# A bf16 matmul of 512 columns behind each aggregation of a graph network's second message stage

## The chip, the core and the metric

The kernel runs on one core of a Trainium2 chip. A core has five engines with instruction streams of their own: TensorE (PE, matrix products into PSUM), VectorE (DVE), ScalarE (ACT), GpSimd (POOL) and SyncE (SP), and 16 DMA engines that move data between HBM and on-chip memory (SBUF). Engines meet only at semaphores. The metric is the device time of one execution in microseconds (us); the median of three runs is given.

## The reference

Two layers of message passing on a graph of 6250 nodes with 256 features and 106250 edges, sorted by destination. Cut to what matters:

```python
# layer 0: a message network per edge, summed per node, then an update network
msg = silu(concat(h[src], h[dst], w) @ mW1 + mb1)
msg = silu(layer_norm(msg) @ mW2 + mb2)
agg = segment_sum(msg, src, 6250)
x = layernorm(x + x + mlp(concat(x, agg)))
# layer 1: the mean over the incoming edges, one projection
agg = segment_sum(x[src], dst, 6250) / max(count, 1)
x = layernorm(x + relu(agg @ W.T + b))
```

The change lies in layer 1's `segment_sum(x[src], dst)`, the second message stage.

## The kernel before

Edges are cut into 831 tiles of 128 (`TILES`), 832 with padding, and nodes into 50 blocks of 125 (`BLOCKS`, `NB`). Since edges are sorted by destination, a tile touches one block or a few neighbouring ones. Each pair of a tile and a block is a *visit*; there are 880 (`VISITS`), in 220 quads of four (`QUADS`, `QT`). The program runs its stages one after the other: preparation of the index tables, the first message stage (until about 3030 us), the update of the nodes in blocks, the second message stage (about 3290 to 4576 us) and the projection with the last norm.

In the second message stage three engines work in a ring, and all synchronisation is by hand.

- **GpSimd** (L498 to L507) issues one indirect DMA per tile: it gathers 128 rows of `x1_tab` from HBM into one of 64 slots of `ring`. The code is unrolled. From the sixteenth tile on, gather `t` waits on the semaphore `agg` until 15 fewer visits than its number are aggregated: `pool.wait_ge(e[1]["agg"], tile - (RING - BEHIND) + 1)`. GpSimd can so be about 15 tiles ahead.
- **PE** (`aggregate`, L720 to L738) loads four slot numbers into registers, waits for the one-hot matrices of the quad (`hot`) and for the quad's four gathers (`s_ring`), and then, for each visit `u` of the quad, waits until VectorE has emptied PSUM bank `u` of the visit four places back (`acc`) and multiplies the one-hot matrix `same1` (128 edges x 125 nodes, fp32) with the gathered rows (128 x 257, fp32, the last column is a one that counts edges). This matmul releases `agg`. In the trace one such fp32 matmul is two MATMUL instructions, so L736 has 1760 of them for 880 visits. The loop of the chip's program holds four quads.
- **VectorE** builds the next quad's four one-hot matrices (`one_hot_1`, L1328), reads four block numbers into registers, and then for each visit waits for `agg` and adds the PSUM bank to the rows of that block in SBUF (`accumulate`, L1341), which releases `acc`.

PSUM has eight banks of 512 fp32 columns. The stage uses banks 0 to 3 for the four visits of a quad. Bank 6 (`PK`) is used in earlier stages and by nobody in this one. `identh` is a 128 x 128 identity matrix in bf16, filled at the start of the program. ScalarE does nothing in this stage.

Of the kernel before, what the change touches and what calls it, by code (L numbers as in the profile page):

```python
# [17 lines left out]
P = 128  # L18
# [3 lines left out]
QT = 4  # L22
# [27 lines left out]
def gnn(nc, x, src, dst, edge_w, mW1, mb1, ln_g, ln_b, mW2, mb2, uW1, ub1, uW2, ub2, W, b, out):  # L50
# [11 lines left out]
    with ExitStack() as ctx:  # L62
        def sb(name, shape, dt=f32):
            return ctx.enter_context(nc.sbuf_tensor(name, shape, dt))
# [6 lines left out]
        identh = sb("identh", [P, P], bf16)  # L71
# [138 lines left out]
        ps = ctx.enter_context(nc.psum_tensor("ps", [P, 7, 512], f32))  # L210
        psh = ctx.enter_context(nc.psum_tensor("psh", [P, QT, P], bf16))
        PM, PZ, PP, PK = 0, 2, 4, 6
# [70 lines left out]
        def later(q, n):  # L283

            return not isinstance(q, int) or q >= n
# [225 lines left out]
        def _(pe):  # L511
# [31 lines left out]
            for c in range(CHUNKS):  # L543
                pe.wait_ge(s_done_g, c + 1)
                for v in range(2):
                    last = nc.tensor.matmul(ps[:, v, 0:HV], onesf[:, :], pick[:, c % 2, 0, v * HV:(v + 1) * HV],
                                            start=c == 0, stop=c == CHUNKS - 1)
# [4 lines left out]
            for c in range(CHUNKS):  # L552
                pe.wait_ge(s_pick, 2 * (c + 1))
                for a in range(3):
                    edges = ends[:, a, c, :] if a < 2 else loaded[:, 2, c, :]
                    for v in range(2):
                        last = nc.tensor.matmul(ps[:, 2 * a + v, 0:HV], edges, pick[:, c % 2, 0, v * HV:(v + 1) * HV],
                                                start=c == 0, stop=c == CHUNKS - 1)
# [166 lines left out]
            def aggregate(q, k_):  # L725

                par = k_ % 2
                pe.load(slot_regs, vslot[0:1, bass.ds(q * QT, QT)])
                at = [pe.snap(reg, min_val=0, max_val=RING - 1) for reg in slot_regs]
                pe.wait_ge(e[1]["hot"], q + 1)  # L730
                if not isinstance(q, int) or q < TILE_QUADS:
                    pe.wait_ge(s_ring[k_], (q // 4 + 1) * (16 * QT))
                for u in range(QT):
                    if later(q, 1):
                        pe.wait_ge(e[1]["acc"], (q - 1) * QT + u + 1)
                    nc.tensor.matmul(ps[0:NB, u, 0:CW], same1[:, par, u, :],  # L736
                                     ring[:, bass.ds(at[u], 1), :].rearrange("p a c -> p (a c)"),
                                     start=True, stop=True).then_inc(e[1]["agg"], 1)  # L738
            pe.wait_ge(s_slots, 5)
            pe.wait_ge(s_ones, 1)  # L740
            for q in range(4):
                aggregate(q, q)
            with pe.Fori(1, TILE_QUADS // 4) as it:
                for k_ in range(4):
                    aggregate(it * 4 + k_, k_)
            for q in range(TILE_QUADS // 4 * 4, QUADS):
                aggregate(q, q % 4)
# [649 lines left out]
```

## Time and profile before

| | |
|---|---|
| median of 3 runs | 4703.93 us |
| lowest and highest run | 4698.99 and 4730.17 us |
| the profiled execution's own time | 4717.16 us |
| its span, first to last instruction | 4715.4 us |
| PE busy | 3347.0 us (71%) |
| VectorE busy | 2799.7 us (59%) |
| GpSimd busy | 3095.4 us (66%) |
| ScalarE busy | 1598.1 us (34%) |

A row of the profile's trace names a line of the kernel, an engine and an operation, with the tiles it writes and reads (`ps<-arena`: PSUM from SBUF; the big arrays all lie in `arena`). PEld is PE's weight load, which runs beside its matmuls. An engine's name with a q (DVEq) is its sequencer: register operations, waits and branches. Such rows are not counted as busy time. "idle before" is the time the engine stood still ahead of an instruction, and the arrow behind it names what ended it; "issue" there means that no wait which the profile shows ended it. Matmuls overlap in the array, so the duration of one is longer than its share of the time. The granted clock is the share of 2.4 GHz that TensorE was given; its two levels are 0.5 and 1.0.

### The profile page before, as it was taken

How to read it: one execution, taken by the hardware profiler on the slowest of the kernel's cores; microseconds unless marked ns; L12 is line 12 of the kernel's file. 1: busy time of each engine (PE TensorE's matmuls, PEld its weight loads, DVE VectorE, ACT ScalarE, POOL GpSimd, SP SyncE). 2: the span in 40 equal slices, each digit the busy share in tenths (PEclk: the TensorE clock that was granted, in tenths of full speed). 3: DMA queues.
4: the chain of work that ended last, by engine and by line, in shares of the span. 5: the costliest groups of instructions: out<-in, count | busy, mean ns of one | idle time of the engine just before them, and what ended most of it. 6: DMA issues, size and time to landing. Idle time of an engine off the chain costs nothing. (4 is left out here: it accounts for less than half of the span.)

```text
span 4715.4 us, 78508 instructions
## 1 busy us (share of the span) xinstructions
PE 3347.0 (71%) x16589; PEld 2444.8 (52%) x16590; DVE 2799.7 (59%) x13402; ACT 1598.1 (34%) x2993; POOL 3095.4 (66%) x2666
## 2 busy tenths in 40 slices
PE   6777777878887777787778777695555555555564
PEld 3366666666666666666666666574222323223232
DVE  4466666666666666666666666577444444444466
ACT  0355555555555545555555555431000000000001
POOL 0078888888888788878887888612666666666620
PEclk8988899898888988989898888897666676666688
DMA  8345555555555555555555555654333233323213
GB/s 278 100 78 83 83 82 83 83 84 82 83 83 83 82 83 82 83 83 83 82 83 82 83 83 83 123 162 135 88 87 87 85 89 88 89 86 90 86 45 100
DMA packets 311717, 437.83 MB, mean 93 GB/s; under 512 B 49696, under 2 KB 256636, under 8 KB 311420
## 3 DMA queue, kind: packets, MB, share of 16 engines
q0 software_dynamic: 208896, 339.90, 38.6%
q1 hardware_dynamic: 102524, 95.40, 6.8%
q14 instruction: 285, 2.33, 0.2%
q8 instruction: 12, 0.20, 0.0%
HBM read 273.86 MB, written 161.01 MB: 92 GB/s over the span
## 5 line engine op out<-in xcount | busy, mean ns | idle before, releaser
L475 POOL DMA_INDIRECT sum<-arena,sidx x880 | 1403.1, 1594 | 304.2 <-issue 258.8
L463 POOL DMA_INDIRECT arena<-p_tab,idx x880 | 863.2, 981 | 489.7 <-issue 254.4
L736 PE MATMUL ps<-arena 128*125 x1760 | 721.2, 547 | 611.0 <-DVE arena L1341 323.9
L504 POOL DMA_INDIRECT arena<-x_tab,esrc x832 | 796.6, 957 | 500.4 <-PE ps L736 222.3
L648 PE MATMUL ps<-w,arena 128*128 128x256 f32 x3520 | 885.0, 384 | 15.6 <-issue 7.6
L736 PEld LDWEIGHTS ps<-arena 128*125 128x125 f32 x1760 | 391.1, 255 | 941.1 <-issue 892.2
L1341 DVE TENSOR_TENSOR arena<-ps,arena 125x257 f32 x880 | 375.0, 426 | 600.0 <-issue 419.4
L613 PE MATMUL ps<-arena 128*128 128x256 f32 x1760 | 607.2, 506 | 109.1 <-ACT arena L840 106.8
L648 PEld LDWEIGHTS ps<-w,arena 128*128 128x128 f32 x3520 | 601.0, 191 | 149.0 <-issue 25.6
L822 ACT ACTIVATE arena<-ps,key 128x128 f32<-128x128 f32 x880 | 251.5, 369 | 1130.8 <-remote 1081.9
L623 PE MATMUL ps<-ident,arena 128*128 128x128 f32 x1760 | 280.0, 310 | 457.1 <-DVE arena L1173 404.2
L613 PEld LDWEIGHTS ps<-arena 128*128 128x128 f32 x1760 | 434.2, 259 | 222.5 <-issue 145.0
L900 ACT ACTIVATE arena<-ps 128x250 f32<-128x250 f32 x50 | 19.0, 382 | 1418.0 <-PE ps L756 1418.0
L623 PEld LDWEIGHTS ps<-ident,arena 128*128 128x128 f32 x1760 | 218.9, 157 | 493.0 <-DVE arena L1173 347.2
L1150 DVE BATCH_NORM_STATS2 bst<-arena 128x6 f32<-128x256 f32 x880 | 330.7, 418 | 236.4 <-ACT arena L812 204.6
L636 PE MATMUL ps<-arena 128*128 x2640 | 361.6, 291 | 5.7 <-DVE arena L1140 4.9
L1140 DVE TENSOR_TENSOR arena<-ps,arena 128x512 f32<-128x512 f32 x440 | 281.3, 679 | 141.2 <-PE ps L623 59.5
L833 ACT ACTIVATE arena<-ps,gb 128x512 f32<-128x512 f32 x440 | 341.8, 777 | 0.0
L1173 DVE TENSOR_SCALAR arena<-arena,mom,nwt 128x256 f32<-128x256 f32 x880 | 321.0, 426 | 34.8 <-DVE nwt L306 26.5
L636 PEld LDWEIGHTS ps<-arena 128*128 128x128 bf16 x2640 | 279.8, 106 | 100.0 <-issue 29.8
L812 ACT ACTIVATE arena<-arena 128x512 f32<-128x512 f32 x440 | 276.7, 629 | 46.3 <-DVE arena L1140 46.1
L1328 DVE TENSOR_SCALAR arena<-nodes,vloc 128x125 f32<-128x125 bf16 x880 | 202.8, 299 | 121.1 <-issue 66.3
(175 smaller groups left out, 4285.7 us busy)
## 6 DMA issues: line engine op xcount, KB each, us to landing
sum<-zeros SPq DMA_DIRECT2D x4, 6400.0 KB
arena<-sum SPq DMA_DIRECT2D x200, 128.0 KB, 2.1
arena<-p_tab,idx POOLq DMA_INDIRECT x880
sum<-arena,sidx POOLq DMA_INDIRECT x880
arena<-x_tab,esrc POOLq DMA_INDIRECT x832
arena<-x_tab SPq DMA_DIRECT2D x50, 128.0 KB, 2.0
pxin<-in_x_dram SPq DMA_DIRECT2D x50, 112.0 KB
p_tab<-prow SPq DMA_DIRECT2D x50, 112.0 KB
```

The source lines that it names most:

```text
L463: pool.indirect_dma_start(out=gat[:, par, u, 0:D], out_offset=None, in_=p_tab[:, :], in_offset=bass.IndirectOffsetOnAxis(ap=idx[:, par, u: ...
L475: pool.indirect_dma_start(out=sums[u][:, :], in_=tot[:, par, u, :], in_offset=None, out_offset=bass.IndirectOffsetOnAxis(ap=sidx[:, par, u ...
L504: pool.indirect_dma_start(out=ring[:, tile % RING, 0:D], out_offset=None, in_=x1_tab[:, :], in_offset=bass.IndirectOffsetOnAxis(ap=esrc[:, ...
L613: last = nc.tensor.matmul(ps[:, PM + u // 2, u % 2 * D:(u % 2 + 1) * D], same[:, par, u, :], msg[:, par, u, 0:D], start=True, stop=True)
L623: last = nc.tensor.transpose(ps[:, PZ + h, u * P:(u + 1) * P], act[:, par, u, h * P:(h + 1) * P], ident[:, :])
L636: last = nc.tensor.matmul(ps[:, PP + u // 2, u % 2 * D:(u % 2 + 1) * D], hott[:, par, u, :], big[:, bass.ds(blocks_[u], 1), i, :].rearrang ...
L648: nc.tensor.matmul(to, zt[:, par, h, u * P:(u + 1) * P], w2[:, h, :], start=h == 0, stop=False)
L736: nc.tensor.matmul(ps[0:NB, u, 0:CW], same1[:, par, u, :], ring[:, bass.ds(at[u], 1), :].rearrange("p a c -> p (a c)"), start=True, stop=T ...
L833: nc.scalar.activation(zt[:, par, h, :], ps[:, PZ + h, :], ACT.Identity, bias=gb[:, h, 1:2], scale=gb[:, h, 0:1]).then_inc(s["zev"], 1)
L1150: nc.vector.bn_stats(bst[:, par, u, :], act[:, par, u, :]).then_inc(s["bst"], 1)
L1173: last = nc.vector.tensor_scalar(act[:, par, u, :], act[:, par, u, :], m[:, 4, u:u + 1], nwt[:, par, 3, u:u + 1], ALU.subtract, ALU.mult)
L1341: nc.vector.tensor_tensor(row, ps[0:NB, u, 0:CW], row, ALU.add).then_inc(s["acc"], 1)
```

## The change

Behind the aggregation of each visit PE runs one more matmul. Its stationary operand is `identh`, its moving operand is `identh` read four times over (512 columns, bf16), and it writes all of PSUM bank 6, which nothing in this stage reads or writes otherwise. It waits for no semaphore and releases none. The aggregation's own release of `agg` stays where it was, ahead of it. Everything else is as it was.

```diff
                     nc.tensor.matmul(ps[0:NB, u, 0:CW], same1[:, par, u, :],
                                      ring[:, bass.ds(at[u], 1), :].rearrange("p a c -> p (a c)"),
                                      start=True, stop=True).then_inc(e[1]["agg"], 1)
+                    nc.tensor.matmul(ps[:, PK, :], identh[:, :], identh[:, :].unsqueeze(1).to_broadcast([P, QT, P]),
+                                     start=True, stop=True)
```

On PE, inside a quad of the second message stage, the program reads as follows (ISA rows are register operations and waits, `arena` is the one-hot matrix and the ring). Before:

```order
L728 TENSOR_LOAD vslot
L729 ISA
L736 ISA [waits e1_acc,s_ring1,e1_hot]
L736 MATMUL ps<-arena 125x257
L736 ISA [waits e1_acc]
L736 MATMUL ps<-arena 125x257
```

And with the change, where L739 is the added matmul:

```order
L728 TENSOR_LOAD vslot
L729 ISA
L736 ISA [waits e1_acc,s_ring1,e1_hot]
L736 MATMUL ps<-arena 125x257
L739 MATMUL ps<-identh 128x512
L736 ISA [waits e1_acc]
L736 MATMUL ps<-arena 125x257
L739 MATMUL ps<-identh 128x512
```

Each pair of a wait and an aggregation has one matmul more behind it, ahead of the wait for the next visit's bank. No other engine's instructions move.

## Rows read from the trace of the kernel before

**Rows 1.** The page: span; granted clock in tenths, 40 slices.
```profile
span 4715.4 us, 78508 instructions
...
PEclk8988899898888988989898888897666676666688
```

**Rows 2.** Stretches of the run: length, busy time (count) by engine, granted clock, DMA share, GB/s.
```profile
3290.00:4522.00 1232.00, 677.13 (x1626) 369.38 (x1627) 526.19 (x1628) 0.00 (x0) 787.01 (x823) 0.68 0.30 88
4523.00:4576.00 53.00, 39.30 (x125) 18.47 (x123) 38.29 (x123) 0.00 (x0) 0.50 (x1) 0.99 0.02 4
```

**Rows 3.** The line view of L736: durations min/median/max, then waits.
```profile
L736 PE MATMUL ps<-arena x1760: 377/534/790, 3285.9 to 4574.7; 128*125 x196
...
  DVE arena L1341: 323.9, 161
...
  POOL arena L504: 222.3, 269
```

**Rows 4.** The line view of L504 (the gathers of the stage).
```profile
L504 POOL DMA_INDIRECT arena<-x_tab,esrc x832: 951/957/1043, 3279.0 to 4522.5; - x167
...
  PE ps L736: 222.3, 269
```

**Rows 5.** The line view of L1341; DVEq is VectorE's sequencer.
```profile
L1341 DVEq FUSED_REGOPS  x880: 2/57/1410, 3292.8 to 4576.4; - x176
L1341 DVE TENSOR_TENSOR arena<-ps,arena x880: 421/426/429, 3292.9 to 4576.5; 125x257 f32 x176
...
  issue: 419.4, 369
```

**Rows 6.** Timeline, a fast stretch: start, duration, engine, line, count, idle before.
```profile
3811.44 9.39 PE L736 MATMUL ps<-arena 128*125 x24 [1.77 <-DVE arena L1341]
...
3814.19 0.95 POOL L504 DMA_INDIRECT arena<-x_tab,esrc  x1 [0.30 <-issue]
3814.26 0.43 DVE L1341 TENSOR_TENSOR arena<-ps,arena 125x257 f32 x1 [0.27 <-issue]
...
3815.45 0.96 POOL L504 DMA_INDIRECT arena<-x_tab,esrc  x1 [0.31 <-PE ps L736]
...
3817.65 0.43 DVE L1341 TENSOR_TENSOR arena<-ps,arena 125x257 f32 x1 [0.28 <-issue]
```

**Rows 7.** Timeline, the slow stretch that follows.
```profile
3825.08 0.42 DVE L1341 TENSOR_TENSOR arena<-ps,arena 125x257 f32 x1 [3.27 <-issue]
...
3825.66 1.21 PE L736 MATMUL ps<-arena 128*125 x2 [4.83 <-issue]
...
3827.19 0.43 DVE L1341 TENSOR_TENSOR arena<-ps,arena 125x257 f32 x1 [1.68 <-issue]
...
3829.28 0.43 DVE L1341 TENSOR_TENSOR arena<-ps,arena 125x257 f32 x1 [1.67 <-PE ps L736]
3829.51 0.95 POOL L504 DMA_INDIRECT arena<-x_tab,esrc  x1 [1.77 <-PE ps L736]
```

**Rows 8.** Stretches: three cycles, each a fast stretch and the slow one after it.
```profile
3808.60:3831.40 22.80, 14.32 (x34) 8.29 (x34) 10.22 (x32) 0.00 (x0) 14.32 (x15) 0.65 0.29 83
3952.70:3976.30 23.60, 14.56 (x34) 7.91 (x32) 10.13 (x32) 0.00 (x0) 15.28 (x16) 0.64 0.30 86
3831.40:3847.40 16.00, 7.38 (x20) 4.50 (x19) 7.09 (x22) 0.00 (x0) 10.51 (x11) 0.71 0.32 95
```

**Rows 9.** Stretches: the matmuls of L736 alone, inside one fast stretch.
```profile
3811.40:3817.00 5.60, 5.56 (x13) 4.21 (x14) 0.50 0.28 83
3817.50:3820.40 2.90, 2.79 (x10) 1.34 (x9) 1.00 0.33 105
```

**Rows 10.** Line view of L636 (bf16, 256 columns), one quad; its stretch.
```profile
L636 PE MATMUL ps<-arena x12: 272/272/273, 507.1 to 508.3; 128*128 x12
...
506.50:508.60 2.10, 1.46 (x12) 1.18 (x12) 0.99 0.40 105
```

**Rows 11.** A stretch after the last gather.
```profile
4530.00:4570.00 40.00, 29.00 (x94) 13.47 (x92) 29.11 (x95) 0.00 (x0) 0.00 (x0) 1.00 0.00 0
```

## The prediction

> **What bounds the kernel now.** I first located the stage, then asked who waits for whom in it, then looked at a timeline to see in what rhythm the waits come. The page gives a span of 4715.4 us and a row of granted clock whose digits are 8 and 9 up to the last third and 6 and 7 through the second message stage [rows 1]. The stage runs from about 3290 us. Until the last gather at 4522.5 us it takes 1232 us, and then 53 us more [rows 2]. In the 1232 us no engine is full: PE is busy 677 us, VectorE 526 us and GpSimd 787 us, at a mean clock of 0.68.
>
> The three engines form a ring. GpSimd issues 832 gathers, from 3279.0 to 4522.5 us, each 0.957 us long [rows 4]. Back to back they start 1.26 us apart (3814.19 and 3815.45) [rows 6], so unhindered they would need 832 x 1.26 = 1048 us. They take 1243.5 us, 1.495 us each, and GpSimd spends 222.3 us waiting for PE [rows 3, 4]. PE in turn waits 323.9 us for the accumulation of L1341 [rows 3]. What the accumulation waits for is the point of the case: of VectorE's idle time before it, 419.4 us is put down to "issue", that is, to nothing the profile shows as a wait, and its sequencer's register operation, 57 ns in the median, takes up to 1410 ns [rows 5].
>
> The timeline shows two alternating states. In a **fast stretch** a quad of four tiles takes VectorE 3817.65 - 3814.26 = 3.39 us, 0.85 us a tile, and PE runs without a break for 9.39 us [rows 6]. In a **slow stretch** accumulations of 0.43 us start 2.1 us apart (3825.08, 3827.19, 3829.28), though the matmul for each was long done; GpSimd streams on until its credit of slots is used up and then stands idle for 1.77 us [rows 7]. After such a pause VectorE is fast again. Why its sequencer slows I can't tell from this trace. What I can read is what it costs on average: three whole cycles, of 22.8, 23.6 and 16.0 us, hold 15, 16 and 11 gathers [rows 8], which makes 1.52, 1.48 and 1.45 us a gather. A short cycle and a long one cost the same per tile. So I treat about 1.5 us a tile as the stage's pace, set between VectorE's sequencer and GpSimd, and not by PE.
>
> **What the change adds.** One matmul and one weight load behind each of the 880 aggregations, nothing removed, nothing moved, no wait, no DMA. The nearest row for the matmul is the bf16 matmul of 256 columns in the first message stage: at a clock of 0.99 twelve of them start within 1.2 us (507.1 to 508.3), 0.11 us apart [rows 10]. 512 columns are then 0.22 us at full clock. The granted clock has two levels here, 1.2 and 2.4 GHz, so at the lower one it is 0.43 us. Its weight load stands beside the stream in those same rows, so I put it at nothing; if it does not hide, it is up to 0.1 us a tile more, and the cover below has room for that.
>
> The aggregation itself: at 0.50 of the clock 13 matmuls (two make one tile) fill 5.56 us, 0.43 us each, 0.86 us a tile; at full clock at most 2.79 / 10 = 0.28 us each, 0.56 us a tile, and that with waits in it [rows 9]. With the added matmul PE needs 0.86 + 0.43 = 1.29 us a tile at the lower clock and at most 0.56 + 0.22 = 0.78 us at the upper one.
>
> Term 1, PE's time. 0.68 of the clock means that (0.68 - 0.5) / 0.5 = 36% of the stage is at the upper level, so the mean price is 0.36 x 0.22 + 0.64 x 0.43 = 0.35 us, times 880 = 312 us of engine time. PE has 1232 - 677 = 555 us idle before the last gather [rows 2]. It fits. If the idle time went away, the 312 us would lie open, but the next terms say where it could.
>
> Term 2, fast stretches at the upper clock: 0.78 us is under VectorE's 0.85. Nothing.
>
> Term 3, fast stretches at the lower clock. 1.29 us is more than 0.85, so here PE takes over from VectorE. After a slow stretch PE starts at 0.50 of the clock and stays there for about 6 us (3811.4 to 3817.0 is at 0.50, 3817.5 on at 1.00) [rows 9]. That is 7 tiles, each 0.43 us later: 3.0 us a cycle. With three cycles of 20.8 us in the mean there are 1232 / 20.8 = 59 of them, 177 us in all, if nothing takes it up.
>
> What takes it up: GpSimd is ahead of PE. Gather t waits only for aggregation t - 15. At 1.29 us a tile PE is just about as fast as GpSimd's 1.26, so GpSimd isn't starved in those 6 us; it merely keeps less credit for the slow stretch that follows, uses it up sooner, pauses sooner, and the pause is what ends the slow stretch. The cycle gets shorter, and the cost per tile does not depend on its length [rows 8]. The pace of 1.5 us also stays above 1.29. The spread between the three cycles, 1.45 to 1.52, is 5%, so it can hide some of a loss; I take a tenth of the 177 us, 17 us, as not absorbed, and keep 0 and 177 as bounds.
>
> Term 4, slow stretches. VectorE takes 2.1 us a tile and PE, at 0.50, has 1.21 us of visible matmul time per tile there [rows 7]; 1.21 + 0.43 = 1.64 is still under 2.1. Since four PSUM banks let PE run four tiles ahead, the added matmul isn't in the loop. Nothing.
>
> Term 5, after the last gather: 94 matmuls in 40 us at clock 1.00, that is 0.85 us a tile, VectorE busy 29.1 of 40 us [rows 11]. PE's 0.78 fits. At most a cold first quad, 4 x 0.43 = 2 us. I take 1.
>
> **Sum.** 0 + 17 + 0 + 1 = 18 us, call it 16 to 20. The profiled execution took 4717.2 us (span 4715.4); the median of the runs shown is 4703.9, 13 us less. Against the median: 4704 + 16 = 4720 us. One per cent, 47 us, is what I count as a difference that a measurement can tell.
>
> **Rivals.**
> *The slow stretches keep their length (slower).* Place: the first six microseconds of each fast stretch. If a slow stretch ends after a fixed time, or needs a pause of GpSimd that comes no sooner, term 3 isn't absorbed: 177 us, 4881 us; half of it, 4793 us. It decides from the point at which GpSimd's wait for PE grows from 222 us. For it: PE is really over VectorE's pace there, 1.29 to 0.85. Against: the three cycles' equal price, and GpSimd's lead. Chance 0.28 for anything over 47 us.
>
> *An even pace (faster).* At 1.29 us PE would hold VectorE near GpSimd's own rhythm, and if VectorE's sequencer only slows after it has run 0.85 us a tile beside a streaming GpSimd, slow stretches get rarer. The limit is 832 x 1.29 = 1073 us instead of 1243.5, so -170 us, 4534 us; half, 4619 us. Against: the clock rises after 6 us and PE is then fast again. Chance 0.12.
>
> *The clock (faster).* In a slow stretch the clock falls, and the next fast one begins at 0.50 [rows 9]; the added columns might keep it up. Then the 1.21 us per tile of slow stretches would be nearer to 1.21 - 0.43 = 0.78. With some 3 such tiles in each of 59 cycles, and if all of it were in the loop, 59 x 3 x 0.43 = 76 us, 4628 us. Against: with VectorE at 2.1 us a tile and PE four tiles ahead it is not in the loop, and in fast stretches PE's 0.86 cold equals VectorE's 0.85. The Trainium skill ("TensorE: Matmul & The Clock Gate", "Why this matters for your kernels") says that gaps between matmul bursts throw PE back to the lower clock, and advises to keep it busy. By that rule the added matmul makes the aggregations faster; the trace agrees about the clock (0.50 after a slow stretch) and speaks against the gain. Chance 0.08.
>
> That the matmul doesn't run at all is excluded by the program's order, where it stands behind every aggregation.
>
> **Chances and range.** My forecast, within 1%: 0.52. Slower 0.28. Faster 0.12 + 0.08 = 0.20. The time is that of the forecast, 4720 us. The range reaches down to the half of the even pace, 4620 us, and up to 0.8 of term 3 unabsorbed, 4704 + 142 = 4846, say 4850 us; about 0.08 lies below and 0.10 above. The forecast's own range is 4690 to 4750 us.
>
> **What would show it.** Right: 880 matmuls of 512 columns; fast stretches that begin at 1.29 us a tile at 0.50 of the clock; cycles shorter than 20.8 us with about 1.5 us a gather; GpSimd's wait for PE near 222 us; the gathers' first to last start near 1243 us; 0.85 us a tile after the last gather. Wrong, slower: the same 10 us slow stretches behind longer fast ones, and PE waiting for VectorE less while GpSimd waits for PE more. Wrong, faster: few accumulations 2 us apart, and gathers 1.26 to 1.3 us apart throughout. A clock near 1.0 in the whole stage with the same time would show the clock's rival to be about the clock alone.

## The result, and the profile after

The changed kernel takes 4661.5 us (median of 4 runs, 4658.0 to 4663.4) against 4704.3 us before: 0.990 of it, 95% interval 0.987 to 0.993. That is 43 us, 0.9 to 1.0%, faster. I had forecast 4720 us and no change. The time lies inside the wide range (4620 to 4850 us), by the room that the rivals had been given, and outside the forecast's own 4690 to 4750 us; the direction was clear of noise and I had missed it. Measured again, on a later occasion, it was 4684.6 against 4718.3 us, 0.993 (0.992 to 0.995).

The profiled execution's span fell by 56 us, from 4715.4 to 4659.4 us. The line view of the gathers says where it went; columns as in [rows 4].

```profile
L504 POOL DMA_INDIRECT arena<-x_tab,esrc x832: 947/953/1040, 3266.0 to 4470.1; - x167
...
  issue: 194.2, 628
  remote: 137.9, 74
  PE ps L736: 79.4, 129
```

The gathers' first to last start now takes 4470.1 - 3266.0 = 1204.1 us, where it took 1243.5: 39 us, 1.449 us a gather instead of 1.495. 13 us were already gone when the first gather started, ahead of anything that the change touches (the profiled execution of before was itself 13 us over the median), and 4 us after the last. So the gain lies where the added matmul lies, ahead of the last gather. The second pair of traces gives 40 us there (1253.0 and 1212.9 us).

The stretch view of the message stage and of its tail, columns as in [rows 2]:

```profile
3277.00:4470.00 1193.00, 792.41 (x2451) 464.11 (x2450) 523.77 (x1633) 0.00 (x0) 784.03 (x823) 0.77 0.31 90
4471.00:4523.00 52.00, 42.95 (x180) 26.73 (x179) 37.73 (x121) 0.00 (x0) 0.02 (x1) 0.99 0.03 4
```

The line view of the added matmul, columns as in [rows 3]:

```profile
L739 PE MATMUL ps<-identh x880: 377/379/634, 3273.9 to 4520.7; 128*128 128x512 bf16 x176
```

PE's busy time and its clock rose (0.68 to 0.77) and the tail after the last gather kept its length [rows 2]. What the added matmul costs PE came out as estimated. A timeline at 0.5 of the clock shows it, columns as in [rows 6]:

```profile
3720.12 0.63 PE L739 MATMUL ps<-identh 128*128 128x512 bf16 x1
3720.55 1.07 PE L736 MATMUL ps<-arena 128*125 x2
3721.40 0.63 PE L739 MATMUL ps<-identh 128*128 128x512 bf16 x1
...
3722.68 0.63 PE L739 MATMUL ps<-identh 128*128 128x512 bf16 x1
```

One tile takes PE 3722.68 - 3721.40 = 1.28 us (I had 1.29), and the added matmul 3720.55 - 3720.12 = 0.43 us. At full clock (0.98 from 3683.0 to 3685.6) a tile takes 3685.13 - 3684.48 = 0.65 us (rows below; I had at most 0.78).

The reader should now compare what VectorE's accumulation waits for with [rows 5]:

```profile
L1343 DVEq FUSED_REGOPS  x880: 3/57/1410, 3279.9 to 4522.0; - x176
L1343 DVE TENSOR_TENSOR arena<-ps,arena x880: 416/426/429, 3280.0 to 4522.2; 125x257 f32 x176
...
  remote: 214.5, 76
  PE ps L736: 206.2, 250
  issue: 136.7, 211
```

"issue" fell from 419.4 to 136.7 us, and "remote", 14.2 us before, is 214.5 us. Part of that is a matter of records: the trace of before holds 677 updates of the semaphore `agg` for its 880 visits, that of after 791, and where the update has no record the profile can name nobody and says "issue". The timeline shows what hides behind "remote":

```profile
3684.05 0.60 PE L736 MATMUL ps<-arena 128*125 x2
...
3684.48 0.38 PE L739 MATMUL ps<-identh 128*128 128x512 bf16 x1
...
3685.13 0.38 PE L739 MATMUL ps<-identh 128*128 128x512 bf16 x1
...
3685.92 0.42 DVE L1343 TENSOR_TENSOR arena<-ps,arena 125x257 f32 x1 [2.34 <-issue]
...
3687.44 0.42 DVE L1343 TENSOR_TENSOR arena<-ps,arena 125x257 f32 x1 [1.10 <-PE ps L736]
...
3688.03 0.69 PE L736 MATMUL ps<-arena 128*125 x2 [0.61 <-issue]
...
3690.97 0.42 DVE L1343 TENSOR_TENSOR arena<-ps,arena 125x257 f32 x1 [3.10 <-remote]
3691.09 0.95 POOL L504 DMA_INDIRECT arena<-x_tab,esrc  x1 [2.17 <-remote]
```

Counted by visits, the accumulation at 3690.97 belongs to the aggregation at 3684.05, not to the one at 3688.03: PE runs up to four visits ahead. That aggregation ended at 3684.65 us. VectorE was free at 3687.87 and starts at 3690.97, 6.3 us after its matmul's end, and GpSimd, whose gather at 3691.09 waits for the same count of `agg`, goes on together with it. The records of the semaphore tell why: four updates stand at 3690.83, 3690.89, 3690.94 and 3690.99 us and none in the 3.5 us ahead of them. **PE's releases arrive late and in a group**, those of four matmuls that ended between 3684.65 and 3688.72, at both receivers together. (The ends of matmuls are modelled by the profile; their starts are recorded.)

Before, the same kind of pause was VectorE's own. In the slow stretch of [rows 7] this gather started 2.5 us ahead of the accumulation at 3829.28:

```profile
3826.79 0.95 POOL L504 DMA_INDIRECT arena<-x_tab,esrc  x1 [0.30 <-issue]
```

By its number it waits for one visit more than that accumulation. So the release had arrived by then, and VectorE alone was late, with a register operation of 0.71 us in the time.

To measure both I took, from the records of each run, every accumulation that started more than 0.4 us after all that it needs by the program: the end of its aggregation's matmul, and the accumulation before it plus what VectorE's other instructions take. Where a register or wait instruction of VectorE lasted over 0.6 us in that time, the delay is put down to VectorE's sequencer, otherwise to a late release. Such sums are in no view of the profile; the tables below give them. They hang on details of the rule: counted without any allowance for VectorE's usual register operations, they are about a tenth larger (515 and 33 us before, 276 and 226 us after).

| kernel | VectorE's sequencer, us | late release, us | sum, us | gathers, first to last, us |
|---|---|---|---|---|
| before | 460 | 41 | 501 | 1243.5 |
| after | 247 | 203 | 450 | 1204.1 |

213 us went from the first column, 162 us came back in the second, 51 us stayed as a gain, of which 39 show in the gathers. One wait took the place of another and left a tenth of it.

The gathers give a second way to part the delays, without durations of register operations: if the gather that waits for the same count had started more than 0.3 us ahead of the delayed accumulation, the release had arrived and VectorE alone was late. The last column counts places where three or four updates of `agg` follow one another within 90 ns each. All of it is counted from the traces and in no view; the runs below the second line are explained in the experiments.

| kernel | delays over 0.4 us, us | VectorE alone late, us | releases in groups of three or four |
|---|---|---|---|
| before, and again | 547 and 544 | 501 and 499 | 1 and 1 |
| after, and again | 501 and 508 | 91 and 127 | 82 and 85 |
| 1024 columns | 490 | 0 | 99 |
| two of 16 columns | 520 | 0 | 100 |
| metronome | 424 | 399 | 0 |

Without stalls the delays are 0 to 9 us, and no two updates of `agg` are closer than 0.5 us (`e4_fill256`, `h1_tiny` and `j2_after`). So part of what the first table puts down to VectorE's sequencer in the kernel after waited for a release as well, and the exchange is nearly whole: with two added matmuls per tile VectorE is never late alone, and all that is left waits for releases that come in groups.

### The profile page after: what moved, and what is told of

Its sections match the earlier page's. It is cut to its first block, busy times and chain, and to the rows that moved or that the text cites. A ratio compares the mean times of both kernels' runs of the same rounds, so it can differ in the third digit from the quotient of the medians.

```text
span 4659.4 us, 80268 instructions
## 1 busy us (share of the span) xinstructions
PE 3475.4 (75%) x17469; PEld 2556.3 (55%) x17470; DVE 2785.1 (60%) x13402; ACT 1594.7 (34%) x2993; POOL 3089.3 (66%) x2666
## 4 chain that ended last, share of the span: by engine, by line
issue 21%; PE 20%; another core or an unknown queue 14%; POOL 14%; DVE 12%; ACT 8%; DVEq 4%; SPq 4%; DMA 2%; ACTq 0%; POOLq 0%
PE ps L736 10%; POOL sum L475 9%; POOL arena L463 5%; PE ps L739 3%; ACT arena L824 2%; PE ps L690 2%; DVE arena L1343 2%; DMA sum<-arena,sidx 2%; ACT arena L814 2%; ACT arena L835 2%; PE ps L613 2%; DVE nwt L303 1%; DVE nwt L300 1%; SPq L345 1%
## 5 line engine op out<-in xcount | busy, mean ns | idle before, releaser
L504 POOL DMA_INDIRECT arena<-x_tab,esrc x832 | 793.5, 954 | 462.6 <-issue 194.2
L736 PE MATMUL ps<-arena 128*125 x1760 | 702.7, 489 | 449.4 <-issue 205.8
L736 PEld LDWEIGHTS ps<-arena 128*125 128x125 f32 x1760 | 391.5, 240 | 750.0 <-issue 683.1
L1343 DVE TENSOR_TENSOR arena<-ps,arena 125x257 f32 x880 | 374.7, 426 | 632.8 <-remote 214.5
L739 PE MATMUL ps<-identh 128*128 128x512 bf16 x880 | 404.8, 460 | 0.0
L636 PE MATMUL ps<-arena 128*128 x2640 | 362.9, 292 | 2.9 <-DVE arena L1142 2.0
L636 PEld LDWEIGHTS ps<-arena 128*128 128x128 bf16 x2640 | 281.3, 107 | 94.2 <-issue 24.0
```

What stands on the lines that cost most here:

```text
L504: pool.indirect_dma_start(out=ring[:, tile % RING, 0:D], out_offset=None, in_=x1_tab[:, :], in_offset=bass.IndirectOffsetOnAxis(ap=esrc[:, ...
L636: last = nc.tensor.matmul(ps[:, PP + u // 2, u % 2 * D:(u % 2 + 1) * D], hott[:, par, u, :], big[:, bass.ds(blocks_[u], 1), i, :].rearrang ...
L736: nc.tensor.matmul(ps[0:NB, u, 0:CW], same1[:, par, u, :], ring[:, bass.ds(at[u], 1), :].rearrange("p a c -> p (a c)"), start=True, stop=T ...
L739: nc.tensor.matmul(ps[:, PK, :], identh[:, :], identh[:, :].unsqueeze(1).to_broadcast([P, QT, P]), start=True, stop=True)
L1343: nc.vector.tensor_tensor(row, ps[0:NB, u, 0:CW], row, ALU.add).then_inc(s["acc"], 1)
```

## The experiments

**Two kinds of occasion.** On one occasion several kernels ran one after the other on the same device, with the kernel before among them. On three occasions the kernel before took 4502 to 4508 us, on the others 4702 to 4723 us, like the runs shown first. Devices number 6 and 2 showed both, so the number does not decide. I call them occasions without and with stalls, and read each kernel against the before of its own occasion.

The two kinds differ in the first message stage too, where it costs next to nothing (the gathers of the second stage start at 3279.0 us in before and at 3268.3 us in `e4_fill256`, a kernel without stalls described below). The stretch views of that stage, `before` and then `e4_fill256`:

```profile
120.00:3000.00 2880.00, 2278.46 (x13240) 1801.08 (x13239) 1894.67 (x10765) 1480.50 (x2724) 2226.33 (x1732) 0.90 0.51 83
```

```profile
120.00:3000.00 2880.00, 2125.39 (x13323) 1633.98 (x13321) 1871.62 (x10824) 1494.58 (x2743) 2234.43 (x1739) 0.99 0.51 84
```

And the same line of VectorE, with what ended its idle time:

```profile
L1140 DVE TENSOR_TENSOR arena<-ps,arena 128x512 f32<-128x512 f32 x440 | 281.3, 679 | 141.2 <-PE ps L623 59.5 <-issue 55.1 <-PE ps L636 14.2
```

```profile
L1142 DVE TENSOR_TENSOR arena<-ps,arena 128x512 f32<-128x512 f32 x440 | 283.4, 686 | 643.3 <-DMA arena<-p_tab,idx 629.1 <-PE ps L636 14.2
```

Without stalls VectorE stands 629 us there for gathers that come too slowly. With stalls that time is used up by longer waits elsewhere (ahead of VectorE's L306 alone 255.2 us against 18.6), the granted clock is 0.90 instead of 0.99, and the trace of before holds records for 9817 of 13426 semaphore updates of this stretch, where one without stalls (`j2_after`) has 13455 of 13493.

### First occasion, without stalls: pace, lead, and dose

`e1_beat`: ScalarE as a metronome for PE.

```diff
+            def beat(q, par):                  # on ScalarE, once per quad
+                for u in range(QT):
+                    ac.wait_ge(e[1]["agg"], q * QT + u + 1)
+                    ...
+                    nc.scalar.activation(w1[0:1024], u1[0:1024], ACT.Copy).then_inc(s_beat, 1)
+                        pe.wait_ge(s_beat, q * QT + u - 1)   # on PE, ahead of the aggregation
```

(The copy's operands are written short; both tiles are free in this stage.)

> No added matmul. ScalarE, idle in this stage, copies 1024 columns of a weight tile that is no longer needed behind each aggregation (about 1.05 us, by 0.63 us for 512 columns in the first stage), and PE waits for the copy of two visits before. PE is so held to about 1.1 to 1.2 us a tile without doing any work in between. Theory A (even pace): it is the slower pace of PE in fast stretches that makes VectorE's slow stretches rarer; then this kernel gains as the change does, 20 to 80 us under before, at a clock no higher than before (0.68 in the stage). Theory B (clock): the added columns keep TensorE's clock up, and the aggregations' shorter duration in slow stretches is the gain; then this kernel gains nothing (0 to +60 us), since the clock stays at 0.6 to 0.7.

Measured: 4522.9 us against 4502.6, ratio 1.005 (1.003 to 1.006).

`e2_credit8`: GpSimd's lead.

```diff
-                if tile >= RING - BEHIND:
-                    pool.wait_ge(e[1]["agg"], tile - (RING - BEHIND) + 1)
+                if tile >= 8:
+                    pool.wait_ge(e[1]["agg"], tile - 8 + 1)
```

> No added matmul. GpSimd may be 8 tiles ahead of the aggregations instead of 15. Theory A: slow stretches need some seven gathers back to back; with 8 tiles of lead GpSimd is tied to PE's rhythm, pauses sooner, and slow stretches get shorter; the time falls by 0 to 60 us or stays, cycles are shorter than 21 us. Theory B: the lead has nothing to do with it, the clock stays 0.68, and less lead only adds waits of PE for gathers: 0 to +100 us.

Measured: 4502.1 against 4502.6 us, ratio 1.000 (0.999 to 1.001).

`e3_fill1024`: the change's two added lines twice.

```diff
+                    nc.tensor.matmul(ps[:, PK, :], identh[:, :], identh[:, :].unsqueeze(1).to_broadcast([P, QT, P]),
+                                     start=True, stop=True)
```

> The change with its added matmul twice: 1024 columns behind each aggregation. PE needs 1.72 us a tile at 0.5 of the clock and about 1.0 us at full clock. Theory A: at the upper clock PE's pace is now 1.0 us, slower than VectorE's 0.85, so the pace gets more even than with one matmul and slow stretches get rarer still, but what runs at 0.5 of the clock is slower than the stage's 1.45 us: 60 us faster to 20 us slower than the change. Theory B: the clock in the stage rises from 0.78 to 0.9 or more and the gain grows with it or stays: 40 to 80 us under before.

Measured: 4505.5 us, ratio 1.001 (1.000 to 1.002).

`e4_fill256`: half the columns.

```diff
-                    nc.tensor.matmul(ps[:, PK, :], identh[:, :], identh[:, :].unsqueeze(1).to_broadcast([P, QT, P]),
+                    nc.tensor.matmul(ps[:, PK, 0:2 * P], identh[:, :], identh[:, :].unsqueeze(1).to_broadcast([P, 2, P]),
```

> The change with half of it: 256 columns behind each aggregation, 1.07 us a tile at 0.5 of the clock and about 0.67 us at full clock. Theory A: PE is slower than VectorE's 0.85 us only at the lower clock, by half as much as in the change; about half of the gain, 10 to 30 us under before. Theory B: the clock is between 0.68 and 0.78 and so is the time, 10 to 30 us under before; the two differ in the length of slow stretches per tile, which A wants shorter in proportion to the pace.

Measured: 4501.1 us, ratio 1.000 (0.999 to 1.001).

None of the four could speak for A or B, because the thing to be explained was absent. The gathers of `e4_fill256`, columns as in [rows 4]:

```profile
L504 POOL DMA_INDIRECT arena<-x_tab,esrc x832: 949/953/1041, 3268.3 to 4315.1; - x167
...
  issue: 161.2, 529
  PE ps L736: 92.0, 302
```

VectorE's accumulation in the same run, its waits as in [rows 5]:

```profile
L1343 DVEq FUSED_REGOPS  x880: 57/57/65, 3282.2 to 4363.3; - x176
...
  PE ps L736: 430.3, 517
```

4315.1 - 3268.3 = 1046.8 us for 832 gathers is 1.26 us each, back to back from first to last. No register operation of the accumulation takes over 0.1 us (the longest of [rows 5] took 1410 ns) and none of VectorE's in the stage over 0.4 us, "issue" and "remote" are gone from its waits, and the two sums of the first table above are 0 and 1 us. GpSimd is the bound, and PE may do as it likes. The 200 us between the two kinds of occasion are the stalls.

### Second occasion, with stalls: the same two kernels

> The kernel before, unchanged, for its trace on the same chip as the others of this call. The first four experiments ran on a chip on which the kernel before takes 4503 us and gathers start 1.26 us apart without a pause. Theory C (the chip): VectorE's slow stretches belong to the chip or the placement of the run, not to the program; then this kernel takes 4503 us on that chip again, with no register operation of VectorE over 0.6 us in the stage. If another chip is given and the slow stretches are back, it takes 4700 us.

> The change, unchanged. Theory C: where slow stretches are absent, GpSimd's gathers are the bound, 832 x 1.26 = 1048 us, and the added matmul changes nothing: within 5 us of before, at a stage clock of 0.85 to 1.0. Where they are present, it is 40 us faster than before, as measured first. Theory B (clock) would have it faster than before on either chip.

Measured: `f1_before` 4724.0 us (one run; the occasion's other runs of before have a median of 4718.3), `f2_after` 4684.6 us, ratio 0.993 (0.992 to 0.995). So the second half of theory C came true: the gain is there where stalls are. Its first half, that they belong to the chip, did not: device 6 had them on the next occasion. Sequencer and late release: 459 and 44 us for `f1_before`, 259 and 197 us for `f2_after`. The shift repeats.

### Third occasion, with stalls: the first experiments again

> ScalarE's copy as a metronome for PE, no added matmul, again, for a chip with slow stretches (before 4700 to 4720 us there). PE is held to 1.26 us a tile or a little less. Theory A (even pace): slow stretches get rarer and the time falls by 20 to 120 us at a stage clock no higher than 0.68. Theory B (clock): no gain, 0 to +60 us, since the clock stays low. On a chip without slow stretches it is 20 us slower than before, as already seen.

Measured: 4722.0 against 4702.2 us, ratio 1.003 (1.002 to 1.005). Slower, where A wanted 20 to 120 us less. PE's tiles started evenly, 1.25 us apart in the median and 1.04 us or more in nine of ten (before: 0.86 and 0.63 us), at a clock of 0.53:

```profile
3290.00:4460.00 1170.00, 893.83 (x1562) 382.47 (x1562) 510.25 (x1561) 825.17 (x781) 752.95 (x788) 0.53 0.30 88
```

Most of the slow sequencer stayed (359 us, late release 40 us). The kernel is not a pure test: it adds a wait per tile on PE, where 69 register or wait instructions between 3300 and 4300 us now take over 0.6 us themselves (none in the kernel before), and instructions on ScalarE, and it lengthens the tail from the last gather to the last accumulation from 54 to 80 us. Its gathers take 1233 us, 10 less than in the trace of before, so an even pace may have a small share; it brings neither the change's 39 us nor its exchange of waits.

> GpSimd's lead cut from 15 tiles to 8, no added matmul, for a chip with slow stretches. Theory A in the form 'a pause of GpSimd ends a slow stretch': GpSimd runs out of credit about 7 tiles sooner, slow stretches shrink from some 10 us to 3 us, cycles from 22 us to 12, and the cost per tile stays 1.5 us or falls: -80 to +20 us. If slow stretches last a fixed time whatever GpSimd does: +50 us or more.

Measured: 4699.6 us, ratio 0.999 (0.997 to 1.000), sequencer 468 us, late release 18 us, gathers 1247.5 us. My idea that a pause of GpSimd ends a slow stretch, and that a shorter lead therefore shortens it, changed nothing.

> The added matmul twice, for a chip with slow stretches. Theory A (even pace): PE at full clock needs 1.0 us a tile, over VectorE's 0.85, so slow stretches get rarer than with one: -50 to -110 us against before. Theory B (clock): clock 0.9 and more, gain 40 to 80 us. The slow stretches' sum (620 us before, 280 to 320 us with the change) tells them apart: A wants it under 250 us.

Measured: 4671.8 us, ratio 0.993 (0.991 to 0.995), a clock of 0.88 in the stage. Sequencer 103 us, late release 348 us. (The 620 and 280 to 320 us of the expectations are from another count, whose rule is not on record; by the tables' rule they are 460 and 247 to 259 us.) The shift went further, the gain did not. The timeline shows the late release without any slow sequencer ahead of it:

```profile
3752.24 1.21 PE L736 MATMUL ps<-arena 128*125 x2 [3.18 <-issue]
...
3755.22 0.42 DVE L1345 TENSOR_TENSOR arena<-ps,arena 125x257 f32 x1 [3.13 <-remote]
3755.35 0.95 POOL L504 DMA_INDIRECT arena<-x_tab,esrc  x1 [2.31 <-remote]
...
3755.80 1.22 PE L736 MATMUL ps<-arena 128*125 x2 [1.49 <-DVE arena L1345]
```

The accumulation at 3755.22 belongs, counted by visits, to an aggregation that ended at 3746.90 us, 8.3 us earlier. The latest one, which ends at 3752.24 + 1.21 = 3753.45 us, is released in the same group, four updates from 3755.09 to 3755.27 us.

`g4_poolpace`:

```diff
+                nc.gpsimd.memset(loc[:, 0, :], 0.0).then_inc(s_pace, 1)
+                pool.wait_ge(s_pace, tile + 1)
                 pool.indirect_dma_start(
```

> No added matmul. GpSimd clears a tile of 4 columns behind each wait and waits for it before it issues the gather, so that gathers start at least some 1.4 to 1.6 us apart instead of 1.26. Theory D (streaming): VectorE's sequencer slows only after about seven gathers 1.26 us apart; spaced out, as in the first message stage (8 indirect DMAs in 13 us, no slow stretch), it never does. Then there are no slow register operations in the stage and it takes 832 times the new spacing: at 1.4 us 1165 us, 80 us under before, at 1.5 us the same as before. If VectorE's slow stretches come from something else, they stay and the time rises by the added spacing, 50 to 150 us.

Measured: 4731.2 us, ratio 1.006 (1.004 to 1.008). The clear cost only 0.09 us, so gathers started at least 1.35 us apart instead of 1.26, less than I wanted. At that spacing the sequencer's sum is 459 us, as before. It speaks against D as far as it goes; a spacing of 1.5 us was not tried.

### Fourth occasion, without stalls

`h1_tiny`: two added matmuls of 16 columns.

```diff
-                    nc.tensor.matmul(ps[:, PK, :], identh[:, :], identh[:, :].unsqueeze(1).to_broadcast([P, QT, P]),
-                                     start=True, stop=True)
+                    nc.tensor.matmul(ps[:, PK, 0:16], identh[:, :], identh[:, 0:16],
+                                     start=True, stop=True)
+                    nc.tensor.matmul(ps[:, PK, 0:16], identh[:, :], identh[:, 0:16],
+                                     start=True, stop=True)
```

> The change with two added matmuls of 16 columns instead of one of 512: as many instructions as the kernel with 1024 columns, but next to no time on PE, so no slower pace and no higher clock. Theory E (instructions): what moves the waiting from VectorE's sequencer to PE's late releases is the number of PE's instructions; then, where slow stretches exist, it does as the 1024 columns did, 20 to 45 us under before, VectorE's slow stretches near 100 us in sum. Theory A/B (columns, by pace or clock): no gain, within 10 us of before, slow stretches near 620 us. Where none exist: within 5 us of before.

Measured: 4503.1 against 4501.7 us, ratio 1.000 (0.999 to 1.001).

`h2_more`: six small instructions more on VectorE per quad.

```diff
+                for i in range(6):
+                    last = nc.vector.memset(scr[:, 0, i:i + 1], 0.0)
+                last.then_inc(s_more, 1)
```

> Before, with six clears of one column each behind the one-hot matrices of a quad: 6 instructions on some 26 to 30 of VectorE's per quad, at some 0.06 us each 0.36 us a quad or 80 us of VectorE time, hidden while the stage takes 1.5 us a tile. Theory F (VectorE's instruction count sets the slow stretches): where they exist, the gathers' 200 us over 1.26 us apiece grow by a fifth or more: +40 to +120 us. If the count is without effect: within 15 us. Where none exist: +0 to +10 us, in the last 53 us of the stage alone.

Measured: 4502.7 us, ratio 1.000 (0.999 to 1.001).

`h3_fewer` (from before) and `h4_fewer_fill` (from the change):

```diff
-                for u in range(QT):
-                    last = nc.vector.tensor_scalar(same1[:, par, u, :], nodes[:, :], vloc[:, bass.ds(q * QT + u, 1)],
-                                                   None, ALU.is_equal)
-                last.then_inc(s["hot"], 1)
+                nc.vector.tensor_tensor(same1[:, par, :, :], nodes[:, :].unsqueeze(1).to_broadcast([P, QT, NB]),
+                                        vloc[:, bass.ds(q * QT, QT)].unsqueeze(2).to_broadcast([P, QT, NB]),
+                                        ALU.is_equal).then_inc(s["hot"], 1)
```

> Before, with a quad's four one-hot matrices made by one tensor_tensor of 500 columns instead of four tensor_scalars of 125: 3 instructions and 3 register operations fewer per quad, of some 26 to 30, and some 0.2 to 0.3 us less VectorE time. Theory F: -20 to -80 us where slow stretches exist. Otherwise within 15 us. Where none exist: 0 to -6 us.

> h3_fewer with the change's added matmul. Theory F with the measured gain of the change: both gains add, -60 to -110 us where slow stretches exist; if both draw on the same waits, it is no better than the better of the two. Where none exist: 0 to -6 us.

Measured: 4516.5 us, ratio 1.003 (1.002 to 1.004), and 4533.3 us, ratio 1.007 (1.005 to 1.009). Fewer instructions made it slower, against both expectations; it goes with slower gathers (last section). Neither was run where there are stalls.

### Fifth and sixth occasion

With stalls:

> Two added matmuls of 16 columns behind each aggregation, again. Where slow stretches exist (before 4700 to 4720 us): theory E (PE's instructions) 20 to 45 us under before with VectorE's slow stretches near 100 us in sum; theories A and B (columns) within 10 us of before, slow stretches near 620 us. Where none exist (before 4502 us): within 5 us, as seen.

Measured: 4694.5 against 4722.6 us, ratio 0.994 (0.992 to 0.996). Without columns worth the name the gain is 28 us, and the shift is as with 1024 columns: sequencer 112 us, late release 366 us. The accumulation's waits, columns as above:

```profile
L1345 DVEq FUSED_REGOPS  x880: 4/57/700, 3292.6 to 4553.8; - x176
...
  remote: 332.2, 105
...
  issue: 72.8, 201
```

The same run's stretch view, its clock third from the end:

```profile
3290.00:4460.00 1170.00, 738.12 (x3157) 496.48 (x3155) 500.76 (x1580) 0.00 (x0) 757.25 (x795) 0.72 0.31 89
```

Its clock is 0.72, `g3_fill1024` had 0.88, the gains are 28 and 30 us. This is the run that decides between columns and instructions, for two added matmuls; for the change's single one the run was missed (below).

> Six one-column clears more on VectorE per quad, again. Where slow stretches exist: theory F (VectorE's instruction count) +40 to +120 us; without effect within 15 us. Where none exist: within 5 us, as seen.

Measured: 4739.7 us, ratio 1.005 (1.004 to 1.007), 17 us instead of at least 40; sequencer 457 us, late release 50 us, as before. The sign is F's, but the sums of the stalls don't grow; I take F as not shown.

Without stalls, `j1_tiny1` (one matmul of 16 columns, as many instructions as the change) beside the change:

> The change with 16 columns in place of 512: the same number of instructions on every engine. Theory E (PE's instructions): where slow stretches exist, the same as the change within 15 us, some 25 to 40 us under before, VectorE's slow register operations halved as in the change (280 to 320 us in sum). If the columns matter: 0 to 15 us under before. Where none exist: within 5 us of before.

> The change, unchanged, beside it: 34 to 43 us under before where slow stretches exist, as twice measured; within 5 us of before where none exist (not yet run there with 512 columns, 256 and 1024 were -1.5 and +3 us).

Measured: 4507.5 and 4505.5 against 4508.3 us, ratios 1.000 (0.999 to 1.001) and 0.999 (0.998 to 1.000). The change itself brings nothing where there are no stalls. Its line views there:

```profile
L504 POOL DMA_INDIRECT arena<-x_tab,esrc x832: 950/957/1043, 3270.3 to 4319.1; - x167
...
  issue: 142.8, 469
  PE ps L736: 110.2, 362
```

And the change's accumulation there:

```profile
L1343 DVEq FUSED_REGOPS  x880: 57/57/65, 3284.2 to 4368.5; - x176
...
  PE ps L736: 482.6, 730
```

All occasions with stalls together (gathers as in each run's own trace; of before there are two traces with stalls):

| kernel | ratio to before | PE instructions added per tile | clock in the stage | sequencer, us | late release, us | gathers, us |
|---|---|---|---|---|---|---|
| before | 1 | 0 | 0.68 | 460 | 41 | 1243.5 |
| before, again | 1 | 0 | 0.69 | 459 | 44 | 1253.0 |
| change, first | 0.990 | 2 | 0.77 | 247 | 203 | 1204.1 |
| change, again | 0.993 | 2 | 0.77 | 259 | 197 | 1212.9 |
| 1024 columns | 0.993 | 4 | 0.88 | 103 | 348 | 1211.1 |
| two of 16 columns | 0.994 | 4 | 0.72 | 112 | 366 | 1222.5 |
| metronome | 1.003 | 1, a wait | 0.53 | 359 | 40 | 1233.0 |
| lead 8 | 0.999 | 0 | 0.70 | 468 | 18 | 1247.5 |
| GpSimd's clear | 1.006 | 0 | 0.68 | 459 | 46 | 1258.3 |
| six clears on VectorE | 1.005 | 0 | 0.70 | 457 | 50 | 1267.1 |

Read it by rows: the split between sequencer and late release goes with the number of added matmuls and weight loads on PE (0, 2, 4), not with clock, columns or pace. And all three kinds of kernel that have the shift gain, no other by more than 3 us. That PE's instructions and not the columns do it is shown with two added matmuls; how they do it is not.

## Why the prediction was wrong, point by point

**What bounds the kernel.** Right in the reading: a ring of three engines, GpSimd's floor of 1.26 us, VectorE's slow sequencer as the thing that costs. The floor is shown by the occasions without stalls, where the gathers take 1046.8 us of the 1048 computed. Wrong in one sentence, and it carried the rest: "I treat about 1.5 us a tile as the stage's pace, set between VectorE's sequencer and GpSimd, and not by PE." I had derived it from three cycles of different length with the same cost per gather. That shows that the cost doesn't hang on the cycle's length. It says nothing about what a new instruction does to it, and PE's instructions turned out to be part of what makes the stalls. One row was also misread: GpSimd's pause of 1.77 us [rows 7] was not used-up credit. Its gather at 3829.51 waits for an aggregation that had ended at 3826.87 us; in before, too, some releases came late.

**Terms 1, 2 and 5** held: the added matmul costs 0.43 us at half clock, PE's tile 1.28 us there and 0.65 us at full clock, the tail has its length (54 us before, 52 us after).

**The step that failed** is that sentence, and with it the bounds of term 3, which knew only a loss, and the "Nothing" of term 4. I expected in term 3 177 us of delay, nearly all absorbed by a pace that stays, 17 us left. The pace did not stay: the gathers took 39 us less, 1.449 instead of 1.495 us each. The term's mechanism, PE over VectorE's pace after a slow stretch, is real (1.28 us a tile), but what decided was outside the term: the delays charged to VectorE's sequencer fell from 460 to 247 us and came back as late releases of PE, 41 to 203 us. That 4661.5 us lies in the stated range is luck: none of the range's terms describes this.

**Term 4.** "In the slow stretches the added matmul isn't in the loop. Nothing." By its time it isn't. By its presence it is: two matmuls of 16 columns do it as well.

**The rivals.** Slower: did not happen, and GpSimd's wait for PE did not grow. It is split otherwise now: 79.4 us to PE and 137.9 us "remote", 217.3 us together, where the line view of before has this beside the 222.3 us of [rows 4], 268.9 us together:

```profile
  remote: 46.6, 41
```

Even pace: the sign was right and the mechanism is not the one, since the metronome holds an even pace, takes 10 us off the gathers and is slower as a whole. Clock: it rose as that rival said, from 0.68 to 0.77. By the rule of the Trainium skill that I had weighed ("TensorE: Matmul & The Clock Gate", section "Why this matters for your kernels"), the matmuls get faster, and the trace agrees about the clock. But the time doesn't follow the clock: 0.88 and 0.72 give the same gain, and without stalls nothing is gained at all.

**What stays open.** Why the two kinds of occasion differ; what the shared thing is through which GpSimd's stream, VectorE's sequencer and PE's releases delay one another, and why two instructions more on PE turn lone delays of VectorE into grouped releases; why VectorE's slow register operations are found in the second message stage alone, although its waits are longer in the first one too; whether the recording of a trace takes part, since every run here has a recorded span and clock; and how much of the change's 34 to 43 us belongs to its columns, since the one-matmul kernel of 16 columns met an occasion without stalls. The intervals of the change (0.987 to 0.993 and 0.992 to 0.995) and of the tiny matmuls (0.992 to 0.996) overlap or touch.

## What to carry to other kernels

Idle time that the profile puts down to "issue" on an engine whose sequencer instructions take ten times their median is a cost of its own: don't treat it as a constant pace that an added instruction on another engine leaves alone, and don't count on it either. Before an effect of one per cent is explained, run the kernel before on several occasions and look whether the very wait that is being explained is there each time; here a 200 us difference between occasions was the larger finding, and the change helps only in one of them. When a wait vanishes, look for the one that has come instead: measure both by the same rule, as a sum, before naming a gain. And match a wait to its own producer by counting, not by what stands nearest in the timeline: here PE ran four visits ahead, and the matmul just before the wait was not the one waited for.

## What the runs showed of the hardware that I had not expected

- The same program has two times, 4502 to 4508 and 4702 to 4723 us, by the occasion. The difference in time lies in one stage, gathers 1.26 against 1.50 us apart; the waits and the clock (0.99 against 0.90) differ in the stage before it as well.
- Releases by PE can arrive several us after the matmul's end, at VectorE and GpSimd at once and up to four together, about 0.05 us apart: 6.3 us for the oldest of a group in the change, 8.3 us with 1024 columns, about 2 us for the newest. Without stalls the sum of such delays is 0 to 17 us.
- A tensor_tensor of VectorE with two operands in SBUF slows the indirect DMAs that GpSimd issues beside it. The gathers of `h3_fewer`, without stalls:

```profile
L504 POOL DMA_INDIRECT arena<-x_tab,esrc x832: 949/953/1446, 3264.9 to 4330.7; - x167
```

Their longest takes 1446 ns where 1040 to 1052 is the longest elsewhere, and first to last they take 4330.7 - 3264.9 = 1065.8 instead of 1046.8 us, 19 us more; the kernel was 15 us slower. Taken one by one, the 301 gathers that overlap such a tensor_tensor in time take 1022 ns in the mean and the other 531 take 953 ns, and each of the 63 over 1.1 us is among the 301. That adds up to 21 us. With the added matmul (`h4_fewer_fill`, 32 us slower) it is 1102 against 953 ns, and the gathers take 1083.4 us; why the matmul adds to it is not shown. The Trainium skill, "SBUF — State Buffer", section "SBUF: two separate sides", says that VectorE and GpSimd share one pair of ports, held for a whole instruction by a VectorE operation with two SBUF inputs against a GpSimd operation that reads SBUF. The measurement agrees in sign and in that the slow gathers are the ones beside the tensor_tensor; that the port is the cause was not isolated here.
